# The edge mask of a windowed attention moved from a DVE operation into TensorE's mask products

## The reference: what is computed

```python
scores = (einsum('bhqd,bkhd->bhqk', q_nope, k_nope)
          + einsum('bhqr,bkr->bhqk', q_rope, k_rope)) * scale   # scale = 1/sqrt(192)
good = (k_ids <= qs) & (k_ids >= qs - LOOKBACK)                 # LOOKBACK = 8
scores = where(good, scores, NEG)                               # NEG = -1e30
attn = softmax(scores, axis=-1)
```

## Time and profile before

| | |
|---|---|
| runs | 820.82, 823.74, 823.79 us |
| profiled execution | 825.13 us, its span 823.2 us |
| PE busy | 754.3 us, 92% of the span |
| DVE busy | 461.5 us, 56% |
| ACT busy | 408.2 us, 50% |
| POOL busy | 188.3 us, 23% |
| setup | 0 to 110.5 us |
| attention blocks | 110.5 to about 588 us |
| steps of blocks 0 to 4 | about 140 to 182, 238 to 274, 334 to 369, 432 to 468, 522 to 556 us |
| feed-forward | about 588 to 823 us |

### The profile page before, as it was taken

How to read it: one execution, slowest core, us unless ns; L and a number is a source line. 1 busy time by engine, 2 the same in 40 slices (tenths; PEclk the granted TensorE clock), 3 DMA queues, 4 the chain that set the end, 5 groups by cost and what they waited for, 6 DMA issues and landing times.

```text
span 823.2 us, 18851 instructions
## 1 busy us (share of the span) xinstructions
PE 754.3 (92%) x7102; PEld 703.3 (85%) x7102; DVE 461.5 (56%) x984; ACT 408.2 (50%) x899; POOL 188.3 (23%) x325
## 2 busy tenths in 40 slices
PE   4899986889999898889899899889999999999997
PEld 4777875769987798779797799778999999999997
DVE  2988763654577345764367545774685263636342
ACT  4788742564446544574355644575588231323231
POOL 2455523433044210533016130422000000000000
PEclk9999996879999899999999899998999999999999
DMA  8899763344322332033320443109120212111021
GB/s 261 260 304 305 248 163 65 80 112 88 71 59 90 78 80 57 26 110 86 66 65 3 123 86 83 34 5 386 65 66 1 59 40 53 43 48 48 15 67 33
DMA packets 46356, 80.89 MB, mean 98 GB/s; under 512 B 5738, under 2 KB 30234, under 8 KB 46282
## 3 DMA queue, kind: packets, MB, share of 16 engines
q1 hardware_dynamic: 40796, 53.34, 25.0%
q0 software_dynamic: 5488, 26.50, 9.4%
HBM read 56.93 MB, written 11.28 MB: 83 GB/s over the span
## 4 chain that ended last, share of the span: by engine, by line
PE 64%; DVE 8%; SPq 5%; issue 3%; ACT 3%; DMA 2%; POOL 1%; DVEq 0%; ACTq 0%; POOLq 0%
PE ps L1335 17%; PE ps L1037 12%; PE ps L907 9%; PE ps L1367 8%; PE ps L1042 6%; SPq L821 5%; PE ps L167 3%; PE ps L980 2%; DVE score L1151 2%; PE ps L953 1%; DVE prob L1175 1%; DMA key_rows<-kv_table,idx 1%; ACT q_lat L1080 1%; PE ps L766 1%; PE ps L1316 1%
## 5 line engine op out<-in xcount | busy, mean ns | idle before, releaser
L1191 DVE TENSOR_TENSOR o_lo<-q_lat,o_hi 128x320 fp32r<-128x320 f32 x80 | 64.6, 813 | 91.0 <-ACT o_hi L1088 88.8
L1037 PE MATMUL ps<-o_hi,wvo_hi 128*128 128x320 f32 x320 | 97.0, 314 | 1.8 <-ACT o_hi L1088 1.8
L1088 ACT ACTIVATE o_hi<-q_lat 128x320 fp32r<-128x320 f32 x80 | 66.9, 842 | 61.1 <-PE ps L1037 60.0
L1037 PE MATMUL ps<-o_hi,wvo_lo 128*128 128x320 f32 x320 | 95.8, 311 | 0.0
L1419 ACT ACTIVATE silu<-ps,ffn_scale 128x320 f32<-128x320 f32 x55 | 29.0, 527 | 97.5 <-PE ps L1335 97.5
L853 POOL TENSOR_TENSOR rot_c<-gathered,cosq 128x192 f32<-128x192 f32 x40 | 27.3, 683 | 213.6 <-PE ps L917 180.1
L1470 DVE SCALAR_TENSOR_TENSOR hidden<-ps,ffn_scale,silu 128x320 f32<-128x320 f32 x55 | 30.2, 549 | 60.5 <-ACT silu L1419 52.9
L1037 PEld LDWEIGHTS ps<-o_hi,wvo_hi 128*128 128x128 f32 x320 | 60.7, 190 | 2.4 <-ACT o_hi L1088 2.1
L1037 PEld LDWEIGHTS ps<-o_hi,wvo_lo 128*128 128x128 f32 x320 | 60.6, 189 | 0.3
L1042 PE MATMUL ps<-o_lo,wvo_hi 128*128 128x320 f32 x320 | 60.4, 310 | 0.0
L487 PE MATMUL ps<-wkv,ctx_hi 128*128 128x384 f32 x192 | 53.4, 388 | 6.4 <-ACT ctx_hi L350 6.4
(11 more groups left out here) (170 smaller groups left out, 1930.6 us busy)
## 6 DMA issues: line engine op xcount, KB each, us to landing
ctx_raw<-ctxT_dram SPq DMA_DIRECT2D x16, 722.0 KB, 7.8
gathered<-key_rows SPq DMA_DIRECT2D x240, 47.2 KB
head_w<-head_w_dram SPq DMA_DIRECT2D x16, 576.0 KB, 5.2
ffn_raw<-ffn_w_dram POOLq DMA_DIRECT2D x11, 768.0 KB, 12.3
kv_table<-tab POOLq DMA_DIRECT2D x16, 288.0 KB, 6.7
rows<-x_dram SPq DMA_DIRECT2D x5, 640.0 KB, 5.2
residual<-x_dram SPq DMA_DIRECT2D x20, 160.0 KB, 2.4
x_rows<-residual SPq DMA_DIRECT2D x20, 160.0 KB, 2.0
```

Source lines behind the costliest of these rows:

```text
L1037: last = pe.matmul(ps[:, 4 + m, 0:TB], w[wt][:, h, cols], o_hi[h % 2][:, :], start=(h == 0 and n == 0), stop=False, skip_group_check=True)
L1088: act.activation(o_hi[h % 2][:, :], q_lat[:, h % 2, :, h // 2], ACT.Copy).then_inc(oh_ok, 1)
L1191: dve.tensor_tensor(o_lo[h % 2][:, :], q_lat[:, h % 2, :, h // 2], o_hi[h % 2][:, :].bitcast(F32), ALU.subtract).then_inc(ol_ok, 1)
```

## The change

The edge mask is no longer added by DVE. It is part of PE's mask product. The moving operand `blocks` gets 27 more rows (3 groups by 9 keys), each with a 1 in the columns of its group and key. The stationary operand becomes a tile of its own per step, `masks[:, s, :]`: the old `other`, plus -1e30 in the new rows where that group's token lacks that key. POOL builds the eight tiles of a block with one operation of 1024 elements per partition, `mask_block`, from `other` and a table `edge` (16 columns per step), each repeated by broadcast. In block 0 this stands behind the second gather, in the others behind the second rotation. PE waits once per block for it (`mask_ok`).

DVE's L1155 goes away. The row maximum and the subtraction read the unscaled scores, and the scale goes into ACT's exponential. The setup makes `edge` from 640 columns of ids in place of `neg_all` from 120 (L394 to L399), and loads `segm` (128 x 640) and a wider `blocks` (128 x 189 in place of 128 x 63).

```diff
+            ("edge", [P, TOK // STEP, SPOTS], BF16),
             ("cosq", [GR, PERIOD * GROUPS, R // 2], F32),
             ("sinq", [GR, PERIOD * GROUPS, R], F32), ("idx_all", [WROWS, BLOCKS * WSETS], I32),
-            ("neg_all", [P, ALLG * WIN], F32),
...
-                for dst, name in ((segw, "segw"), (segh, "segh"), (base, "row_base"), (joff9, "joff9")):
+                for dst, name in ((segw, "segw"), (segm, "segm"), (base, "row_base"), (edge_of, "edge_of")):
...
-                    neg = w["neg_all"][:, :].rearrange("p (g j) -> p g j", j=WIN)
-                    link(dve.tensor_copy(seghf[:, :], segh[:, :]))
-                    link(dve.tensor_tensor(keyh[:, :, :], seghf[:, :].unsqueeze(2).to_broadcast([P, ALLG, WIN]),
-                                           joff9[:, :].unsqueeze(1).to_broadcast([P, ALLG, WIN]), ALU.add))
-                    link(dve.tensor_scalar(neg, keyh[:, :, :], 0.0, float(LK - 1), ALU.max, ALU.min))
-                    link(dve.tensor_tensor(neg, neg, keyh[:, :, :], ALU.not_equal))
-                    link(dve.tensor_scalar(neg, neg, NEG, None, ALU.mult))
+                    link(dve.tensor_copy(wanted[:, :], segm[:, :]))
+                    link(dve.tensor_scalar(wanted[:, :], wanted[:, :], edge_of[:, 0:1], None, ALU.add))
+                    link(dve.tensor_scalar(inside[:, :], wanted[:, :], 0.0, float(LK - 1), ALU.max, ALU.min))
+                    link(dve.tensor_tensor(inside[:, :], inside[:, :], wanted[:, :], ALU.not_equal))
+                    link(dve.tensor_scalar(w["edge"][:, :, :].rearrange("p s x -> p (s x)"), inside[:, :],
+                                           edge_of[:, 1:2], None, ALU.mult))
...
+    masks = sb("masks", [P, STEPS, P], BF16)
...
+        def mask_block(b, first):
+
+            if not first:
+                pool.wait_ge(s_mm, c16(b - 1, 16))
+            pool.tensor_tensor(
+                masks[:, :, :].rearrange("p s (x r) -> p s x r", r=HH),
+                w["edge"][:, bass.ds(b * STEPS, STEPS), :].unsqueeze(3).to_broadcast([P, STEPS, SPOTS, HH]),
+                w["other"][:, :].rearrange("p (x r) -> p x r", r=HH).unsqueeze(1)
+                .to_broadcast([P, STEPS, SPOTS, HH]), ALU.add).then_inc(mask_ok, 1)
...
+                mask_block(0, True)
...
-                for s in range(STEPS):
+                for s in range(2):
+                    rotate(b, s, False)
+                mask_block(b, False)
+                for s in range(2, STEPS):
...
+            if s == 0:
+                pe.wait_ge(mask_ok, c1(b, 1))
...
-                pe.matmul(ps[:, e, 0:GROUPS * GK], w["other"][sides[e], :], w["blocks"][sides[e], :],
+                pe.matmul(ps[:, e, 0:GROUPS * GK], masks[sides[e], s, :], w["blocks"][sides[e], :],
...
-            act.activation(ex[s % 2][:, :, :], sd[s % 2][:, :, :], ACT.Exp).then_inc(s_exp, 1)
+            act.activation(ex[s % 2][:, :, :], sd[s % 2][:, :, :], ACT.Exp, scale=SCALE).then_inc(s_exp, 1)
...
-            dve.scalar_tensor_tensor(
-                out=sa[:, :, :].rearrange("p (e g) j -> p e (g j)", e=2),
-                in0=sc[:, :, :].rearrange("p (e g) j -> p e (g j)", e=2), scalar=SCALE,
-                in1=w["neg_all"][:, bass.ds((b * STEPS + s) * GROUPS * WIN, GROUPS * WIN)].unsqueeze(1)
-                .to_broadcast([P, 2, GROUPS * WIN]),
-                op0=ALU.mult, op1=ALU.add).then_inc(s_scl, 1)
-            dve.wait_ge(s_scl, c8(b, s + 1))
-            dve.tensor_reduce(mx[:, :], sa[:, :, :], AX.X, ALU.max).then_inc(s_max, 1)
+            dve.tensor_reduce(mx[:, :], sc[:, :, :], AX.X, ALU.max).then_inc(s_max, 1)
             dve.wait_ge(s_max, c8(b, s + 1))
-            dve.tensor_tensor(sd[s % 2][:, :, :], sa[:, :, :],
+            dve.tensor_tensor(sd[s % 2][:, :, :], sc[:, :, :],
...
+    edges = np.arange(P) % HALF - GQ
+    edge = (edges >= 0) & (edges < GROUPS * WIN)
+    group, key = np.where(edge, edges // WIN, 0), np.where(edge, edges % WIN, 0)
+    col = np.arange(GROUPS * GK)
+    blocks = np.where((query < GQ) & (query == (col % GK // WIN)[None, :]), f(FAR), f(0))
+    blocks = blocks + (edge[:, None] & (group[:, None] == (col // GK)[None, :])
...
+                       & (key[:, None] == (col % WIN)[None, :]))
+    spot = np.arange(SPOTS) // (GQ + 1) * GQ + np.minimum(np.arange(SPOTS) % (GQ + 1), GQ - 1)
+    edgetok = (np.arange(TOK // STEP)[None, :, None] * STEP + np.array(GSTART)[group][:, None, None]
+               + spot[None, None, :]).reshape(P, -1)
```

More of the change, by code:

```diff
@@ L66 @@
 FAR = -2.0 ** 127
+SPOTS = 2 * (GQ + 1)
 MEANS = WIN
@@ L203, in build_setup @@
             other32 = sb("other32", [P, P], F32, index)
-            blocks32 = sb("blocks32", [P, GK], F32, index)
+            blocks32 = sb("blocks32", [P, GROUPS * GK], F32, index)
         hi.append(sb("ctx_hi1", [P, KC, TROWS], F32R))
@@ L207, in build_setup @@
         tab = [sb(f"tab{i}", [P, KT, ROW]) for i in range(2)]
-        segh = sb("segh", [P, ALLG], I32)
-        seghf = sb("seghf", [P, ALLG])
-        joff9 = sb("joff9", [P, WIN])
-        keyh = sb("keyh", [P, ALLG, WIN])
+        with ExitStack() as plain:
+            segm = sb("segm", [P, TOK // STEP * SPOTS], I32, plain)
+        inside = sb("key_inside", [P, TOK // STEP * SPOTS])
+        wanted = sb("key_wanted", [P, TOK // STEP * SPOTS])
+        edge_of = sb("edge_of", [P, 2])
         zero = sb("zero", [P, KC, TROWS - LK - MEANS])
@@ L415, in index_work @@
                     link(dve.tensor_copy(w["other"][:, :], other32[:, :]))
-                    link(dve.tensor_copy(w["blocks"][:, :].rearrange("p (g k) -> p g k", g=GROUPS),
-                                         blocks32[:, :].unsqueeze(1).to_broadcast([P, GROUPS, GK])))
+                    link(dve.tensor_copy(w["blocks"][:, :], blocks32[:, :]))
                     dve.memset(done_mark[:, :], 0.0).then_inc(index_ok, 1)
@@ L700, in build_attention @@
     sc = sb("score", [P, E, WIN])
-    sa = sb("score_scaled", [P, E, WIN])
+    masks = sb("masks", [P, STEPS, P], BF16)
     mx = sb("score_max", [P, E])
@@ L719, in build_attention @@
     tr_mm, tr_ev = sem("tr_mm"), sem("tr_ev")
-    t_mm, t_ev, s_mm, s_red, s_scl, s_max, s_sub, s_exp, s_sum, s_inv, s_pn, pf_ok = (
-        sem(s) for s in ("t_mm", "t_ev", "s_mm", "s_red", "s_scl", "s_max", "s_sub", "s_exp",
+    t_mm, t_ev, s_mm, s_red, mask_ok, s_max, s_sub, s_exp, s_sum, s_inv, s_pn, pf_ok = (
+        sem(s) for s in ("t_mm", "t_ev", "s_mm", "s_red", "mask_ok", "s_max", "s_sub", "s_exp",
                          "s_sum", "s_inv", "s_pn", "pf_ok"))
@@ L1533, in constants @@
     row = np.arange(P) % HALF // HH
-    rowtok = first[None, :] + (side * GQ + np.minimum(row, GQ - 1))[:, None]
     same = row[:, None] == (np.arange(GK) // WIN)[None, :]
@@ L1538, in constants @@
     other = (query < GQ) & (query != row[None, :])
-    blocks = (query < GQ) & (query == (np.arange(GK) // WIN)[None, :])
-    return wintok, rowtok, {
+    edges = np.arange(P) % HALF - GQ
[8 more added lines that the diff above has]
+               + spot[None, None, :]).reshape(P, -1)
+    return wintok, edgetok, {
         "ident": np.eye(P, dtype=f),
-        "mask": same.astype(f), "other": other.astype(f), "blocks": np.where(blocks, f(FAR), f(0)),
+        "mask": same.astype(f), "other": other.astype(f), "blocks": blocks.astype(f),
         "cosk": cos[kpos], "sink": np.concatenate([-sin[kpos], sin[kpos]], -1),
@@ L1545, in constants @@
         "row_base": (wintok // LQ * TROWS).astype(f),
-        "joff9": np.broadcast_to((np.arange(WIN) - LOOKBACK).astype(f), (P, WIN)),
+        "edge_of": np.stack([key - LOOKBACK, np.where(edge, NEG, 0.0)], 1).astype(f),
     }
@@ L1559, in twice @@
         return np.concatenate([m, m[..., P:]], -1)
-    wintok, rowtok, arrays = constants()
+    wintok, edgetok, arrays = constants()
     seg = np.asarray(itok_BxS_0_1023).reshape(TOK)
@@ L1565 @@
     arrays["segw"] = seg[wintok]
-    arrays["segh"] = seg[rowtok]
+    arrays["segm"] = seg[edgetok]
     arrays["wkvc"] = np.asarray(L0_xattn_W_kvc).reshape(KC, P, KVC).transpose(1, 0, 2)
```

## The result

| | before | changed |
|---|---|---|
| median of the runs, us | 823.76 | 799.53 |
| runs | 820.82 to 829.79 (4) | 798.46 to 800.47 (4) |
| profiled execution (span) | 825.13 (823.2) | 799.19 (797.5) |
| mean granted TensorE clock | 0.955 | 0.979 |
| POOL busy | 188.3 | 196.1 |

The ratio is 0.970, 95% interval 0.964 to 0.975. The direction was right, the size was not.

The account below looks back on a forecast made before the run. DVE's chain was taken to bound part of the steps, PE's rate others, gathered rows block 0. Gains of 7.95 us (5.7, 1.4, 0.25, 0.6) less costs of 2.6 (1.8, 0.8) gave 818.3 us, range 812 to 824.

Parts of the forecast that it names:

- The clock: PE's granted clock around the blocks' ends: 0.6 us gained for one short drop at a block's start.
- Rival 1: A clock drop is spared at the blocks' ends, 3.0 us each in two loop blocks: 812 us; chance 0.20.
- First part: Early steps of blocks 1 to 3, up to the third step's picks: 1.1 us saved per block without L1155.
- Middle: Middle steps of blocks 1 to 3: PE's rate of 3.52 us per step rules, nothing is gained.
- Last part: Last steps of blocks 1 to 3: earlier exponential lets ACT take step 5's values sooner; 0.8 us saved per block.
- Block 4: Steps of block 4, which have no register work: 1.4 us gained together, bounds 0.5 and 2.
- Block 0: Block 0 waits for gathered rows until its last step; only the last window counts, 0.25 us gained.
- The mask operation: POOL's added operation, put at 2.35 us, holds an o_lo; PE stalls 0.45 us, 1.8 in four blocks.
- the forecast's own rule: PE's stall in the output products is the POOL mask operation's time less 1.9 us, and nothing below that.
- Rival 3: POOL's mask operation takes 4.3 us and stalls PE's output products by 2.4 us in four blocks: 826.1 us; chance 0.11.
- Setup: Larger tables loaded ahead of the first rows of x delay them: 0.8 us lost, 1.0 at most.
- Rival 2: The steps are PE's and ACT's anyway: 2.45 us gained against 2.6 of cost, 823.6 us; chance 0.22.

Follow-up runs that it names:

- the filled kernel: The kernel before, with PE's idle time at the ends of blocks 0 to 3 filled with unused fp32 products: 813.48 us, ratio 0.984.
- the kernel with the second half left out: The kernel before without L1155 in the last four of a block's eight steps (4 to 7): 811.65 us, ratio 0.982.
- the kernels with the DVE operation back: The changed kernel plus a DVE operation of L1155's shape adding zeros, from an address worked out per step (824.54 us) or a fixed one (818.62 us).

## Why the prediction was wrong, step by step

Split by cause, the 25.7 us of the profiles are about: 9.9 of DVE's operation itself (2.65 per loop block: 2.58 between the picks, 0.31 behind the last, less 0.24 ahead of the first; 2.0 in block 4), 14.0 of clock (6.3 at the compressions and at the end of block 4, 4.0 left over in the steps, 3.7 in the queries behind the loop edges), 3.4 of shorter gaps, less 1.6 in setup, block 0 and small things. These are two executions. In the changed kernel's other profile the 3.7 behind the loop edges were not saved.

- *The clock* is the step that failed: "I count 0.6 us here for one of the short drops at a block's start and leave the large ones to a rival". It was worth about 14 us. All three large drops of the loop blocks went, and the filled kernel shows the cause, PE's waits in the last steps. Rival 1 named the mechanism and put two drops at 6.0 us, with 0.20. "Against: another idle stretch of 0.8 us stays" was no argument: the stretch stayed (PE waits 0.79 and 0.78 us there now) and the drop didn't. What went was half of the wait of 1.54 us ahead of step 6, which the prediction doesn't list.
- *The loop edge* was in no step. Its gap was on the chain with 3.94 us, more than any single stall that the prediction priced, and its row wasn't read.
- *First part*, 1.1 per block: from the first pick of block 2 to the third, 7.54 - 5.78 = 1.76, near the upper bound of 1.9 that the prediction gave for all stalls gone. L1175's stall went too. Leaving L1155 out in that half alone gave 1.51 over the block.
- *Middle*, 0: right. From the third pick to the fifth 7.17 before and 7.15 changed, and the value products kept 3.52 us.
- *Last part*, 0.8: right in size and in mechanism, by ACT's rows and by the picks (fifth to eighth 11.46 and 10.67). It moved more than itself, as the kernel with the second half left out shows.
- *Block 4*, 1.4: 2.0, the upper bound.
- *Block 0*, 0.25 gained: not to be seen in a stretch that came out 1.2 us later.
- *The mask operation*: mechanism right, size wrong. It took 1.93 us and not 2.35, and the forecast's own rule, time less 1.9, then gives 0.03 us a block in place of 0.45; the held `o_lo` was ready 0.13 us before PE's product. In the kernels with the DVE operation back it cost up to 0.27 us a block. Rival 3 fell with it. The Trainium skill says for a DVE operation with two SBUF inputs that the second one to issue "fully blocks" (SBUF — State Buffer, section "Summary: rules for kernel authors"). DVE's row agrees (2.30 us for an `o_lo` of 0.79), but for its tail: it ended 0.56 us after POOL and not 0.79.
- *Setup*, 0.8: nothing that can be told from the spread. DVE's first statistics came no later; POOL's index copy behind the setup started at 111.06 against 110.75. In the other profiles the setup's compression ended at 111.1 to 111.9 with the old tables (115.2 once) and at 111.5 to 112.0 with the new ones (113.9 once).
- *Rival 2* (steps bound by PE and ACT) is refuted by the picks: 23.59 against 26.17. Its own sum, 2.45 against 2.6, gives 823.9 and not 823.6.

Had the costs been put at 0 and the clock at rival 1's 3.0 for three blocks, the sum would have been 7.35 + 9 = 16.4 us, 807.4; most of the rest is the loop edges (7.1) and the larger first part (2.0), less setup and block 0 (1.5).

## What to carry to other kernels

When a clock drop follows a stretch in which PE waits, the chain that makes it wait is worth its own length plus the whole drop: price the drop first, and test it with useless products in the idle time, which took 13 us off here. Look at every "issue" piece of over a microsecond on the chain, at a loop's start above all, and at which large load runs beside it; the load's place relative to the loop's end is a part of the schedule. Compare several executions before you put a number on it: the kernel before took from 813.74 to 831.49 us, the less the higher its mean clock. And a cost on an engine with slack is paid only when the operation that it holds up ends after its reader wants it: here 0.0 to 0.27 us per block, by how the two met.

## What was not expected of the hardware

- PE's gap at a loop edge ended 2.3 to 3.4 us after an instruction packet on queue 8, in 28 of 28 cases, and lay at 1.25 to 2.14 us when no 640 KB load had been issued, up to 4.29 with one issued 2.6 us ahead.
- The 20 query products behind a gap ran at full clock after all 6 gaps of up to 1.74 us and at half clock after all 8 of 2.40 and more. In between, from 1.79 to 2.14, 6 ran at half and 8 at full clock: half after 1.83, 1.88 and 2.04, full after 1.84, 2.09 and 2.14. So there the gap's length doesn't decide it; what does stays open.
- POOL's bf16 addition of 1024 elements per partition, in runs of 8 and with broadcasts, took 1.93 us alone or with an `o_lo` waiting behind it, 1.7 ns per element behind 0.20 us, where fp32 took 2.08. No run varies type, runs or broadcasts by themselves. Where an `o_lo` was already running when it started, it took 2.33 to 2.40 us.
